# Local attention: every third set of products made by GpSimd, and a rebuilt list schedule

## The reference, cut to what matters

```python
x = x + _L0_attn_a_ref(_layernorm(x, axis=-1), ...)
x = x + _L0_ffn_ref(_layernorm(x, axis=-1), ...)
x = x + _L0_attn_b_ref(_layernorm(x, axis=-1), ...)
x = x + _L0_ffn_ref(_layernorm(x, axis=-1), ...)
```

```python
k_g = k[:, :, idxc]                      # 44 shifted copies of the keys
k_mod = k_g * (1.0 + scale_embed)
scores = jnp.einsum('bhtd,bhtjd->bhtj', q, k_mod) * scale
scores = scores + pos_bias.T[None, :, None, :]
attn = jax.nn.softmax(scores, axis=-1)
out = jnp.einsum('bhtj,bhtjd->bhtd', attn, v_g)
```

## Time and profile before

| | |
|---|---|
| median of 3 runs | 1752.73 us (1747.72 to 1756.09) |
| the profiled execution | 1755.84 us, of which 1753.8 us are the span from first to last instruction |
| PE busy | 1584.8 us, 90% of the span |
| DVE busy | 1278.3 us, 73% |
| ACT busy | 791.3 us, 45% |
| POOL busy | 133.0 us, 8% |
| products on DVE (L1306) | 240 instructions, 400.3 us |

### The profile page before, as it was taken

The page is one execution under the profiler, slowest core; times in us unless marked ns, Lnnn a source line. Parts: engine busy times, 40 slices in busy tenths (PEclk is TensorE's granted clock), DMA queues, the critical chain, the costliest instruction groups (busy, mean ns, idle before and its releaser), DMA issues. The chain is left out here.

```text
span 1753.8 us, 28230 instructions
## 1 busy us (share of the span) xinstructions
PE 1584.8 (90%) x10544; PEld 884.8 (50%) x10560; DVE 1278.3 (73%) x3138; ACT 791.3 (45%) x1474; POOL 133.0 (8%) x155
## 2 busy tenths in 40 slices
PE   5689899998999989999899999999899998997976
PEld 2163564545655465554654556454655446554533
DVE  5968856896588956788568975789667986656723
ACT  1133445535364543644455353544435443553533
POOL 1020110001101020000200001000100001000000
PEclk8998999999999999999999999999999999998988
DMA  9040450014300152020700235001530206004000
GB/s 320 21 158 14 150 153 2 16 73 169 87 2 23 66 181 74 4 86 8 230 19 2 86 108 148 2 15 73 179 76 3 74 27 210 20 20 128 15 1 12
DMA packets 50261, 133.96 MB, mean 76 GB/s; under 512 B 6256, under 2 KB 22576, under 8 KB 45520
## 3 DMA queue, kind: packets, MB, share of 16 engines
q1 hardware_dynamic: 50128, 132.16, 23.2%
HBM read 80.99 MB, written 46.04 MB: 72 GB/s over the span
## 5 line engine op out<-in xcount | busy, mean ns | idle before, releaser
L1306 DVE TENSOR_TENSOR arena_AB<-qT,kT 128x2048 f32<-128x2048 f32 (+3 forms) x240 | 400.3, 1718 | 20.7 <-PE bank L1632 14.3
L1361 DVE CUSTOM_DVE_ANT_0 bank<-bank,causal_b 128x512 f32<-128x512 f32 (+3 forms) x512 | 233.6, 527 | 85.2 <-PE bank L1697 84.6
L1543 PE MATMUL bank<-arena_F,kept 128*128 128x512 f32 x512 | 238.8, 616 | 5.7 <-DVE arena_F L1451 2.9
L1625 PE MATMUL bank<-arena_AB,slot_w 128*32 128x512 f32 x1408 | 200.2, 617 | 42.2 <-DVE arena_AB L1306 40.7
L1135 ACT ACTIVATE arena_AB<-bank 128x512 f32<-128x512 f32 (+1 forms) x352 | 167.7, 596 | 65.8 <-PE bank L1713 65.7
L1168 ACT ACTIVATE arena_F<-bank,kept 128x512 f32<-128x512 f32 x256 | 157.5, 700 | 15.3 <-PE bank L1543 13.5
L1543 PEld LDWEIGHTS bank<-arena_F,kept 128*128 128x128 f32 x512 | 97.4, 197 | 119.5 <-issue 104.4
L1821 PE MATMUL bank<-kept,arena_F 128*128 128x256 f32 x512 | 117.0, 382 | 7.4 <-ACT arena_F L1185 5.5
L1806 PE MATMUL bank<-arena_F,kept 128*64 128x512 f32 x512 | 121.5, 602 | 1.2 <-ACT arena_AB L1135 0.3
L1543 PE MATMUL bank<-cont_hi,by_cont 128*128 128x512 f32 (+1 forms) x272 | 113.9, 419 | 9.4 <-DVE arena_AB L1361 7.2
L1543 PE MATMUL bank<-xnT,kept 128*128 128x512 f32 x256 | 116.4, 604 | 2.3 <-issue 0.9
(11 more groups left out here) (186 smaller groups left out, 2350.3 us busy)
## 6 DMA issues: line engine op xcount, KB each, us to landing
arena_AB<-band SPq DMA_DIRECT2D x32, 1344.0 KB, 7.1
arena_AB<-stacks SPq DMA_DIRECT2D x64, 384.0 KB
stacks<-arena_AB SPq DMA_DIRECT2D x48, 256.0 KB, 2.7
band<-arena_AB SPq DMA_DIRECT2D x32, 328.0 KB, 2.6
stacks<-xnT SPq DMA_DIRECT2D x32, 256.0 KB, 2.5
band<-kT SPq DMA_DIRECT2D x4, 1352.0 KB, 22.2
stacks<-xn SPq DMA_DIRECT2D x16, 256.0 KB, 2.3
kept<-kept_pack SPq DMA_DIRECT2D x1, 3765.0 KB, 18.9
```

Source lines behind the costliest of these rows:

```text
L1306: ins = nc.vector.tensor_tensor(prod[SET_AT[i]][:, col:col + c, :], qT[:, hf, :].unsqueeze(1).broadcast_to([P, c, T]), k, ALU.mult)
L1361: ins = nc.vector.tensor_tensor_reduce(out=s, in0=s, in1=causal[:, (TT - 1 - i) * P:T], scale=-1.0, scalar=BIG, op0=ALU.add, op1=ALU.min, ...
L1543: ins = nc.tensor.matmul(out(ps), w, x, start=n == 0, stop=n == len(pairs) - 1)
L1625: ins = nc.tensor.matmul(ps[HS * col:HS * (col + 1), :], slot_w[:, slot(n), :], prod[SET_AT[i]][:, col, :], start=r == 0, stop=False, skip ...
```

## The change

Sets 2, 5, 8, ..., 23 of each A call (every third, 8 of 24) are made by POOL instead of DVE, into the same buffers and with the same waits. POOL signals them on a semaphore of its own, `pool_made`. The planner's tables get new lengths for many blocks, a POOL length for these sets, other weights, and start times for the x of two more calls.

```diff
+BY_POOL = [q for q in range(len(SETS)) if q % 3 == 2]
...
-        p.put(("prod", q), ("DVE", 0.067 * len(runs(q)) + 0.534 * len(of), *needs), ("PE", 0.86 if r < 3 else 1.12 if g == NG - 1 else 0.98))
+        make = ("POOL", 0.1 + 1.2 * len(of)) if q in BY_POOL else ("DVE", 0.067 * len(runs(q)) + 0.534 * len(of))
+        p.put(("prod", q), (*make, *needs), ("PE", 0.9 if r < 3 else 1.3 if g == NG - 1 else 1.1))
...
-LOAD, CLOCK = 0.1, 0.95
-TICK, DEPTH = 0.02, 1.61
+LOAD, CLOCK = 0.1, 1.0
+TICK, DEPTH = 0.02, 1.28
...
-RELEASE = {(ATTENTION[0], "stats"): 4.2, (ATTENTION[0], "xn"): 7.6, (SETUP, "slots"): 10.2, (SETUP, "small"): 60.0}
+RELEASE = {(ATTENTION[0], "stats"): 4.9, (ATTENTION[0], "xn"): 8.1, (ATTENTION[1], "stats"): 24.0,
+           (ATTENTION[3], "stats"): 30.0, (SETUP, "slots"): 11.5, (SETUP, "small"): 60.0}
...
+        def product_made(u, q):
+
+            if q in BY_POOL:
+                return nth(u, "pool_made", BY_POOL.index(q) + 1)
+            return nth(u, "prod_made", q + 1 - sum(k < q for k in BY_POOL))
...
+            def products(u, i):
+                hf, before = PRODUCTS[SETS[i][0]][0], attention_before(u)
+                if i in FIRST_OF and before and before.stage == "A":
+                    pool.wait_ge(*bank_full(before, ("oT", TT - 1)))
+                if i in FIRST_OF and before and before.stage == "B":
+                    pool.wait_ge(*bank_full(before, ("ST", SET_AT[i], TT - 1, 0)))
+                for x in latest(u, [("qk", hf), ("qk", KD + hf)]):
+                    pool.wait_ge(*bank_read(u, x))
+                if USED_BY[i] is not None:
+                    pool.wait_ge(*products_used(u, USED_BY[i]))
+                for run in runs(i):
+                    out, q, k = product_views(i, run)
+                    ins = nc.gpsimd.tensor_tensor(out, q, k, ALU.mult)
+                ins.then_inc(sem["A"]["pool_made"], 1)
...
-                    pe.wait_ge(*nth(u, "prod_made", i + 1))
+                    pe.wait_ge(*product_made(u, i))
```

More of the change, by code:

```diff
@@ L131, in norm_phases @@
     p.put("pow", ("POOL", 1.0, ("stats", "DVE")))
-    p.put("xn", ("DVE", 1.3, ("pow", "POOL")))
+    p.put("xn", ("DVE", 1.35, ("pow", "POOL")))
     for k in range(KD):
@@ L200, in local_phases @@
                 needs.append(("on", i - 2, "PE"))
-            p.put(("oT", i), ("PE", 1.35 if i > 0 else 0.86, *needs), ("ACT", 0.48))
+            p.put(("oT", i), ("PE", 1.46 if i > 0 else 1.02, *needs), ("ACT", 0.6))
         else:
@@ L225, in raw @@
     def raw(h, n):
-        p.put(("S", h, n), ("PE", (0.22, 0.23, 0.12)[n], ("stack", h // 4, "DMA")), ("DVE", (0.62, 0.76, 0.37)[n]))
+        p.put(("S", h, n), ("PE", (0.2, 0.25, 0.1)[n], ("stack", h // 4, "DMA")), ("DVE", (0.64, 0.76, 0.38)[n]))
     def maxima(hf):
@@ L231, in turn_maxima @@
     def turn_maxima(hf):
-        p.put(("mT", hf), ("PE", 0.24, ("mx", hf, "DVE")), ("ACT", 0.46), ("SP", 0.4), ("DMA", 4.5))
+        p.put(("mT", hf), ("PE", 0.32, ("mx", hf, "DVE")), ("ACT", 0.6), ("SP", 0.4), ("DMA", 4.5))
     def turned_scores(n, m):
@@ L245, in weigh @@
         g, k = STEPS[n]
-        p.put(("PV", n), ("PE", (0.86, 0.64, 0.43, 0.23)[k], *[("ST", n, m, "ACT") for m in range(len(SHARE[k]))],
+        p.put(("PV", n), ("PE", (1.0, 0.78, 0.6, 0.37)[k], *[("ST", n, m, "ACT") for m in range(len(SHARE[k]))],
                           *([("v", m, "DVE") for m in range(2)] if n == 0 else [])))
@@ L281, in expert_phases @@
     p.put("rh", ("PE", 0.46, ("cont", "DVE")), ("ACT", 0.6))
-    p.put("lg", ("PE", 0.9, ("rh", "ACT")), ("DVE", 2.85))
+    p.put("lg", ("PE", 1.0, ("rh", "ACT")), ("DVE", 2.93))
     for kind, n in EXPERTS:
@@ L290, in expert_phases @@
             if n == 5:
-                p.put("ln_b", ("DVE", 1.14, ("xn", "DVE")))
+                p.put("ln_b", ("DVE", 1.25, ("xn", "DVE")))
         elif kind == "gT":
-            p.put(("gT", 0), ("PE", 0.24, ("gates", "DVE")), ("ACT", 0.46))
+            p.put(("gT", 0), ("PE", 0.32, ("gates", "DVE")), ("ACT", 0.7))
         elif kind == "gb":
@@ L298, in expert_phases @@
             needs = [("hid", 4 * n + k, "ACT") for k in range(4)]
-            p.put(("eo", n), ("PE", 1.72, *needs), ("DVE", 0.67 if n == 0 else 1.4, ("gb", n, "ACT")))
+            p.put(("eo", n), ("PE", 1.87, *needs), ("DVE", 0.67 if n == 0 else 1.52, ("gb", n, "ACT")))
     for m in range(KF):
@@ L303, in expert_phases @@
         p.put(("dec", n), ("PE", 3.43, *[("c2s", m, "ACT") for m in range(KF)]), ("DVE", 0.61))
-        p.put(("tanh", n), ("ACT", 0.6, ("dec", n, "DVE")))
-    p.put("stats_2", ("DVE", 1.93, ("tanh", 0, "ACT"), ("tanh", 1, "ACT")))
+        p.put(("tanh", n), ("ACT", 1.1, ("dec", n, "DVE")))
+    p.put("stats_2", ("DVE", 2.1, ("tanh", 0, "ACT"), ("tanh", 1, "ACT")))
     p.put("pow_2", ("POOL", 1.0, ("stats_2", "DVE")))
-    p.put("close", ("DVE", 3.3, ("pow_2", "POOL"), ("ln_b", "DVE")))
+    p.put("close", ("DVE", 3.4, ("pow_2", "POOL"), ("ln_b", "DVE")))
     if layer == 1:
-        p.put("store", ("SP", 0.4, ("close", "DVE")), ("DMA", 4.0))
-        p.put("load", ("SP", 0.4, ("store", "DMA")), ("DMA", 4.0))
+        p.put("store", ("SP", 0.4, ("close", "DVE")), ("DMA", 7.0))
+        p.put("load", ("SP", 0.4, ("store", "DMA")), ("DMA", 5.0))
     return p.table
@@ L423, in between_calls @@
     if u.stage == "A" and prev.stage == "B":
-        if engine == "DVE" and name[0] == "prod" and name[1] in FIRST_OF:
+        if engine in ("DVE", "POOL") and name[0] == "prod" and name[1] in FIRST_OF:
             needs.append((prev, ("ST", TT * SET_AT[name[1]] + TT - 1, 0), "PE"))
@@ L624 @@
     "A": {
-        **NORM, "vs_shifted": 64, "prod_made": len(SETS),
+        **NORM, "vs_shifted": 64, "prod_made": len(SETS) - len(BY_POOL), "pool_made": len(BY_POOL),
         "prod_used": len(SETS) - 2 * NG, "pa_ready": TT,
@@ L1038, in local_attention @@
                     power(u, norms["AB"])
+                elif name[0] == "prod":
+                    products(u, name[1])
                 else:
@@ L1290, in local_attention @@
                 elif kind == "prod":
-                    hf, g, _, r = PRODUCTS[SETS[i][0]]
-                    before = attention_before(u)
+                    hf, before = PRODUCTS[SETS[i][0]][0], attention_before(u)
                     if i == 0 and before and before.stage == "A":
@@ L1296, in local_attention @@
                         dve.wait_ge(*bank_full(before, ("ST", SET_AT[i], TT - 1, 0)))
-                    if g == 0 and r == 0:
-                        for x in latest(u, [("qk", hf), ("qk", KD + hf)]):
-                            dve.wait_ge(*bank_read(u, x))
+                    for x in latest(u, [("qk", hf), ("qk", KD + hf)]):
+                        dve.wait_ge(*bank_read(u, x))
                     if USED_BY[i] is not None:
@@ L1302, in local_attention @@
                     for run in runs(i):
[L1303 to L1307 removed]
+                        out, q, k = product_views(i, run)
+                        ins = nc.vector.tensor_tensor(out, q, k, ALU.mult)
                     ins.then_inc(sem["A"]["prod_made"], 1)
```

39 lines of the change are left out of this document (20 added, 19 removed), and 6 rows, old and new, of the table CALL_PULL.

## The result

The changed kernel takes **1884.9 us**, median of four runs (1881.5 to 1889.9). The kernel before, on the same chip, has 1752.2 us (1747.7 to 1756.1). The ratio is 1.0755, interval 1.0736 to 1.0774: slower by 133 us, above the forecast of 1793, above its own range (1768 to 1828) and above the wider one (to 1850).

The account below looks back on a forecast made before the run. PE was taken as the leading bound, 90% busy, with DVE the bound in A0's products. Terms 14 + 6 + 30 - 10 = +40 us gave 1796 us profiled, 1793 us median; range 1768 to 1828, wider 1738 to 1850.

Parts of the forecast that it names:

- The price of POOL's work: POOL's eight sets a call: 2.2 ns a column, 4.5 us for 2048 columns, 31.5 us a call, bounds 30 to 35.
- The held share: Part of POOL's product time that shuts DVE out of SBUF: 0.9, or 28.4 us a call, against 16.5 us saved.
- A0 and A1: First two calls' products: +14 us in A0 (bounds +2 to +17), +6 us in A1 (bounds 0 to +10).
- some 64: Sign for A0: from first to last product some 64 us instead of 50.5.
- A2 to A7: +5 us a call: Six middle calls: DVE's load fits on average, local clashes cost +5 us each, +30 us in all; bounds 0 and +12.
- the cover: In A2 to A7, sets 2, 14 and 17 on POOL run beside DVE work mostly reading banks, 12 us of cover.
- the cushion: In A2 to A7, PE's four buffers of products and 3.8 us idle in the stretch stand against DVE's delays.
- nothing is covered: Rival, chance 0.15: POOL and DVE alternate through all eight calls with share 1, +120 us less 10, 1863 us.
- The planner's -10 us: Other new planner numbers recover a tenth of PE's 97 us idle outside the products: -10 us, bounds +10 to -30.
- The powers queued behind products: Three powers a call wait behind a POOL product, delaying DVE at L1499 or L1284 by up to 4.5 us more.
- above 1830 if powers' delays ripple into F: Condition for being wrong on size: above 1830 us if the powers' delays ripple into F's expert steps.
- DVE's waits for POOL above 1 us each: Sign for the middle calls: DVE's waits for POOL rise above the present 1 us each.

Follow-up runs that it names:

- e11: Changed kernel with the planner's old numbers and only sets 0 and 1 on POOL: 1825.6 us, 1.0412 against the kernel before.
- e3: Changed kernel, same lists, waits and buffers, but POOL writes constants by two memsets instead of each product, reading nothing: 1721.3 us, 0.9807 against the kernel before.
- e1: Changed kernel with all the planner's new numbers kept, but every set made by DVE and none by POOL: 1781.5 us, 1.0151 against the kernel before.
- e2: Changed kernel with POOL still making the eight sets, but all the planner's old numbers: 1935.3 us, 1.102 against the kernel before.
- e7: Changed kernel with the new numbers, but only sets 14 and 17 on POOL: 1836.4 us, 1.0451 against the kernel before.
- e13: e3 with DVE making the first two products of all its 16 sets a call twice: 1846.4 us, 1.051 against the kernel before.
- e14: e3 with DVE making the first two products of 8 of its 16 sets a call twice: 1783.9 us, 1.0158 against the kernel before.
- e5: Changed kernel replanned with POOL's measured length and a ban on overlapping its products with DVE's SBUF-reading blocks: 1906.3 us, 1.0856 against the kernel before.
- e4: Changed kernel with the new numbers, but only sets 2, 8, 14 and 20 on POOL: 1875.0 us, 1.0673 against the kernel before.
- e12: Changed kernel with the new numbers, but only set 2 on POOL: 1793.1 us, 1.0223 against the kernel before.

## Why the prediction was wrong in size

**The direction and the mechanism held.** Products of DVE and POOL exclude each other over SBUF, bank readers don't take part (L1412 at 425 ns beside POOL, e11's maxima), and the changed kernel without POOL's reads is 164 us faster (e3).

**The price of POOL's work was close.** Forecast: 4.5 us for 2048 columns; measured 3.81, 1.86 ns a column, below my bounds. The held share was forecast at 0.9. Undisturbed, a call's 14336 columns are 26.7 us on POOL; DVE lost 200.8 / 8 = 25.1, or 0.94 of it. So a call costs DVE 25.1 us instead of 28.4, against 16.5 saved: 8 x 8.6 = 69 us, and the page shows 72 more. DVE's mean for 2048 columns is 2.90 us, not above 3 as I had asked for. By the Trainium skill (SBUF — State Buffer, "Who interferes with whom") the lock is for the whole instruction. For products the trace agrees, with the 5.00 us of the row above and the other 18 like it. The power in the earlier trace rows stays the exception: the trace of before has six products that start 0.12 us into one, and none is longer than 2.29 us. The same section names casts and tensor_scalar among the instructions that can take the shared pair, and says that a GpSimd instruction which only writes doesn't hold a two-input product; the CAST at 687 ns beside products at 2286 in e3 agrees with both. I had weighed only the two-input rule.

**A0 and A1 came out right in part by luck.** A2 starts 20.0 us later, +14 and +6 forecast, and A0's products take 65.3 us, "some 64" forecast. But they start 11 us earlier than before and end only 4 later (84.2 instead of 80.5), and with the new numbers they take 61 us even when DVE makes all of them (e1). A1's take 13.9 us more, not 6, above the bound of 10. What the terms describe is seen in e2, with the old numbers: +13 and +7. With the lists of the changed kernel, the reading costs 48 us up to A2, and the new list gives back 28 (e3 against before), a gain that the sum had no term for.

**The step that failed is "A2 to A7: +5 us a call"**, with its bounds of 0 and +12. Measured are 104 us from A2's start to A7's end, 17 a call; on equal lists the reading costs 123 (e3). The upper bound was also added up wrongly: 94.3 + 7.5 - 90.8 is 11, not 12. Three things in it were wrong. First, the cover: sets 2, 14 and 17 were to run beside bank readers. Set 2 came behind the maxima, beside none of them, and met a small CAST (3.78 us in A4), and 14 and 17 don't start where the list has them but when PE frees a buffer, which starts DVE's products too (e7). Second, the cushion: "four buffers and 3.8 us idle", DVE's load "fits on average". e13 and e14 show 0.75 to 0.79 us of kernel for each us of DVE from the first on. I had compared busy times in a stretch; but DVE's idle time there is mostly time in which it waits for PE (12.5 of 14.2 us in e3), as PE does for it. Third, the clock: the sum put at nothing the time at 1.2 GHz behind PE's idle times. It grew from 98 to 233 us and is, by the estimate above, 57 of the 138 us that idling and clock cost together.

**The rival "nothing is covered"** was the nearest: 1863, with the right idea of cover. Its 120 us come from a DVE loss of 15 us a call, where 8.6 was measured, so that its closeness is partly luck too.

**The planner's -10 us** has no single measured value. By way of e2 the split costs +182 and the new numbers give back 50; by way of e1 the numbers cost 28 and the split 103. The term rested on the wrong question: the old list had been fitted to the old split, so each half of the change alone makes it worse. Neither value, -50 or +28, lies within the bounds of -30 and +10.

**The powers queued behind products** did not do what I feared. DVE waits for POOL's rstd_F at L1499 for 9.9 us in ten times, longest 1.1, where it was about 1 us each before. The condition "above 1830 if powers' delays ripple into F" names the wrong cause for a size that came true. "DVE's waits for POOL above 1 us each" was a wrong sign to look for: a stop inside an instruction shows as its length, not as a wait.

**Open** is whether any list makes POOL's products pay. None of the versions in which POOL reads beat the kernel before; e5 tried one rule, without tuning the other numbers. Why e11 lost the rest of its 73 us, and what the new lists of e4, e7 and e12 add to their loss, is open as well.
